# Common up projection for two tiles at a time, and scatter-adds written out with indices read in place

## What is computed

```python
h = patches @ conv_w + conv_b + pos
a = layernorm(h)
h = h + attention(a) + a                 # 12 heads; q and k are layer-normed; softmax
x = layernorm(h)
route_prob = softmax(x @ Ws + bs)        # 9 experts
p, routes = max(route_prob), argmax(route_prob)
out_e = gelu(x @ W1[e] + b1[e]) @ W2[e] + b2[e]          # 192 -> 768 -> 192
common, sel = out_0, out_routes
final = where(routes == 0, common, p * sel + (1 - p) * common)
h = h + final
```

## Time and profile before

| | us |
|---|---|
| median of 3 runs (lowest, highest) | 388.1 (388.03, 388.18) |
| profiled execution, its own time | 386.88 |
| its span in the trace | 385.0 |
| PE busy | 364.3 (95%) |
| POOL busy | 188.3 (49%) |
| DVE busy | 172.2 (45%) |
| ACT busy | 163.9 (43%) |

### The profile page before, as it was taken

One profiled execution on the slowest core, in us unless ns is written; L12 is line 12 of the kernel. 1 busy time (PEld: TensorE's weight loads), 2 busy tenths in 40 slices (PEclk: granted clock), 3 DMA queues, 4 the chain that ended last, 5 costly groups with the idle time before them and its releaser, 6 DMA issues. The chain is left out here.

```text
span 385.0 us, 10445 instructions
## 1 busy us (share of the span) xinstructions
PE 364.3 (95%) x3291; PEld 325.6 (85%) x3292; DVE 172.2 (45%) x595; ACT 163.9 (43%) x553; POOL 188.3 (49%) x307
## 2 busy tenths in 40 slices
PE   6799999999999999899999999998999999999991
PEld 5677877788888888788888899997999999999991
DVE  3365767777777787544232265411112211111111
ACT  0122233333333354778444454335545544555540
POOL 1657977777777787443013006740333333444333
PEclk9999999999999999999999999999999999999997
DMA  7764335353321435435000905626666776676630
GB/s 243 234 207 120 101 105 162 94 156 91 90 79 48 130 113 166 124 97 187 20 0 14 245 2 142 217 80 147 150 170 160 176 187 164 167 165 164 155 76 0
DMA packets 40589, 49.58 MB, mean 129 GB/s; under 512 B 10412, under 2 KB 32313, under 8 KB 40553
## 3 DMA queue, kind: packets, MB, share of 16 engines
q1 hardware_dynamic: 34641, 42.95, 37.8%
q0 software_dynamic: 5024, 5.72, 8.8%
q10 hardware_dynamic: 888, 0.45, 0.4%
HBM read 39.84 MB, written 10.27 MB: 130 GB/s over the span
## 5 line engine op out<-in xcount | busy, mean ns | idle before, releaser
L641 PE MATMUL bank<-W,ARENA 128*128 (+1 forms) x516 | 94.6, 334 | 1.5 <-issue 1.2
L641 PEld LDWEIGHTS bank<-W,ARENA 128*128 128x128 f32 x516 | 82.8, 190 | 5.7 <-issue 1.5
L1371 POOL DMA_INDIRECT out<-ARENA,ID x25 | 39.4, 1575 | 71.3 <-DVE ARENA L1236 62.0
L855 ACT ACTIVATE ARENA<-score_banks,B1R 128x128 f32<-128x128 f32 x150 | 41.5, 376 | 39.8 <-PE score_banks L631 24.1
L855 ACT ACTIVATE ARENA<-score_banks,B1T 128x128 f32<-128x128 f32 x108 | 29.9, 375 | 31.8 <-PE score_banks L631 31.8
L1269 POOL TENSOR_TENSOR VS<-V,R 108x384 f32<-108x384 f32 x32 | 27.7, 865 | 30.5 <-DVE R L960 30.2
L1232 DVE TENSOR_TENSOR ARENA<-bank,B 128x192 f32<-128x192 f32 x25 | 8.9, 358 | 71.6 <-PE bank L641 71.6
L623 PE MATMUL score_banks<-RINGS,W1R 128*128 128x128 f32 x300 | 37.8, 276 | 1.4 <-ACT RINGS L795 0.8
L623 PEld LDWEIGHTS score_banks<-RINGS,W1R 128*128 128x128 f32 x300 | 35.6, 192 | 1.8 <-issue 1.8
L1260 POOL TENSOR_TENSOR RINGS<-QK,GM 128x216 f32<-128x216 f32 x64 | 34.1, 553 | 3.4 <-PE score_banks L579 3.4
L579 PEld LDWEIGHTS score_banks<-QK,RINGS 48*108 48x108 f32 x512 | 28.7, 171 | 6.1 <-issue 2.9
(11 more groups left out here) (149 smaller groups left out, 622.1 us busy)
## 6 DMA issues: line engine op xcount, KB each, us to landing
W1R<-in_w SPq DMA_DIRECT2D x25, 384.0 KB
V<-v_rows SPq DMA_DIRECT2D x96, 54.0 KB
W<-in_w SPq DMA_DIRECT2D x9, 576.0 KB, 4.2
W1R<-in_w_rest SPq DMA_DIRECT2D x50, 96.0 KB
ARENA<-in_patches SPq DMA_DIRECT2D x11, 384.0 KB, 3.6
packed_tokens<-RINGS POOLq DMA_DIRECT2D x1, 2425.0 KB, 13.2
ARENA<-packed_tokens SPq DMA_DIRECT2D x25, 97.0 KB, 2.8
PT<-in_patches SPq DMA_DIRECT2D x6, 384.0 KB, 3.2
```

Source lines behind the costliest of these rows:

```text
L641: last = pe.matmul(bank[2 * par][:, 0:D], HT[par][:, c * P:c * P + P], W2[:, bass.ds((expert * FC + c) * D, D)], start=c == 0, stop=c == F ...
L855: last = act.activation(HT[par][:, to:to + P], bank[6 + g][:, c * P:c * P + P], ACT.Gelu, bias=b1[:, bias:bias + 1])
L1371: pool.indirect_dma_start(out, bass.IndirectOffsetOnAxis(ap=ID[par][:, 0:1], axis=0), YR[par], None, bounds_check=TOKENS - 1, oob_is_err=F ...
```

## The change

From tile 4 on the common up projection works on pairs of tiles (2q, 2q+1), q = 2 to 8, in the even steps 24, 26, ..., 36. Each matmul then has 256 moving columns, the two tiles' rows side by side, for one load of weights. The results take six half banks in banks 4 to 7. In the odd steps 25, 27, ..., 37 there is no up projection. `gelu_pair` takes 256 columns in each of six activations, into buffers twice as long; `common_down` still works on one tile at a time, at its old step. `count_ranks` uses bank 3 in place of banks 4 and 5 and keeps its place. The arena that holds the buffers grows by 112 columns. In the groups' part, POOL's loop is written out, the copy to `ID` and its two waits are gone, and the indirect DMA reads the token numbers from `SLOT_ROWS` directly.

```diff
+PAIR = 2
+ALONE = 4
+ARENA_COLS = 5912
-        ID = [sb(f"ID{i}", 1, I32) for i in range(2)]
-        HT = [cut(DFF) for _ in range(2)]
+        HTP = [cut(PAIR * DFF) for _ in range(2)]
+        HT = [HTP[1][:, i * DFF:(i + 1) * DFF] for i in range(2)]
+        def xn2t_pair(q):
+            both = QK[:, 2 * TOKENS:4 * TOKENS].rearrange("p (u n) -> p u n", u=PAIR)
+            return both[:, :, q * 2 * P:(q + 1) * 2 * P]
+        def pair_chunk(c):
+            b, at = ((bank[6], 0), (bank[6], 1), (bank[4], 0), (bank[7], 0), (bank[7], 1), (bank[5], 0))[c]
+            return b[:, at * PAIR * P:(at + 1) * PAIR * P]
...
 -                ffn_down(n, n % 2, 0)
+                if n < ALONE:
+                    ffn_down(n, n % 2, 0)
+                    return
+                q, u = n // PAIR, n % PAIR
+                for c in range(FC):
+                    if c % (FC // 2) == 0:
+                        pe.wait_ge(gelu_done, 4 * q + 2 + 2 * (c // (FC // 2)))
+                    last = pe.matmul(bank[2 * u][:, 0:D], HTP[q % 2][:, (c * PAIR + u) * P:(c * PAIR + u + 1) * P],
+                                     W2[:, c * D:(c + 1) * D], start=c == 0, stop=c == FC - 1)
+                last.then_inc(y_done, 1)
+            def pair_up(q):
+                pe.wait_ge(gelu_done, 4 * q)
+                pe.wait_ge(s_shifted, STEPS)
+                pe.wait_ge(xn2t_saved, PAIR * q + 2)
+                for c in range(FC):
+                    pe.matmul(pair_chunk(c), W1[:, c * P:c * P + P], xn2t_pair(q)[:, :, 0:P],
+                              start=c % 3 != 1, stop=False, skip_group_check=True)
+            def pair_up_rest(q):
+                for c in range(FC // 2):
+                    at = DFF + c * P
+                    for g in range(2):
+                        rows = slice(g * DB, g * DB + DB)
+                        last = pe.matmul(pair_chunk(g * (FC // 2) + c), W1[rows, at:at + P], xn2t_pair(q)[rows, :, P:2 * P],
+                                         start=False, stop=True, skip_group_check=True)
+                        if c == FC // 2 - 1:
+                            last.then_inc(f1_done, PAIR)
 ...
-                pe.wait_ge(s_shifted, STEPS)
-                pe.matmul(bank[4][:, 0:TE], const("before"), onehot, start=True, stop=True)
-                pe.matmul(bank[5][:, 0:TE], const("ones"), onehot, start=True, stop=True).then_inc(ranks_done, 1)
+                pe.wait_ge(o_copied, STEPS)
+                pe.matmul(bank[3][:, 0:TE], const("before"), onehot, start=True, stop=True)
+                pe.matmul(bank[3][:, 2 * P:2 * P + TE], const("ones"), onehot, start=True, stop=True).then_inc(ranks_done, 1)
 ...
-                if kf is not None:
+                if kf is not None and kf < ALONE:
                     common_up(kf)
+                elif kf is not None and kf % PAIR == 0:
+                    pair_up(kf // PAIR)
 ...
+            def gelu_pair(q):
+                act.wait_ge(y_done, PAIR * q - 2)
+                for g in range(2):
+                    act.wait_ge(f1_done, 4 * q + 2 * g + 2)
+                    for c in range(g * (FC // 2), (g + 1) * (FC // 2)):
+                        last = act.activation(HTP[q % 2][:, c * PAIR * P:(c + 1) * PAIR * P], pair_chunk(c), ACT.Gelu,
+                                              bias=B1T[:, c:c + 1])
+                    last.then_inc(gelu_done, PAIR)
 ...
-            def group_step(i, ks):
-                kh, = ks
-                n, par, half = tile_at(i, kh)
-                if kh >= 2:
-                    pool.wait_ge(y_added[par], 16 * half)
-                pool.tensor_copy(ID[par][:, :], SLOT_ROWS[:, bass.ds(2 * n + 1, 1)].bitcast(I32)).then_inc(id_ready, 1)
-                pool.wait_ge(id_ready, n + 1)
-                pool.wait_ge(y_scaled, n + 1)
-                ride(pool)
-                pool.indirect_dma_start(out, bass.IndirectOffsetOnAxis(ap=ID[par][:, 0:1], axis=0), YR[par], None,
-            two_by_two(pool, group_step, (0,), GROUPS)
+            for n in range(GROUPS):
+                pool.wait_ge(y_scaled, n + 1)
+                ride(pool)
+                row_ids = SLOT_ROWS[:, 2 * n + 1:2 * n + 2].bitcast(I32)
+                pool.indirect_dma_start(out, bass.IndirectOffsetOnAxis(ap=row_ids, axis=0), YR[n % 2], None,
```

More of the change, by code:

```diff
@@ L135, in const @@
             return CST[0:rows, a:b]
-        ARENA = sb("ARENA", 5800)
+        ARENA = sb("ARENA", ARENA_COLS)
         marks = [0]
@@ L143, in cut @@
             marks[0] += n
-            assert marks[0] <= 5800
+            assert marks[0] <= ARENA_COLS
             return ARENA[:, a:a + n]
@@ L717, in main_step @@
                     conv(kc, KC // 2, KC)
-                if kf is not None:
+                if kf is not None and kf < ALONE:
                     ffn_up_rest(kf, xn2t(kf), W1)
+                elif kf is not None and kf % PAIR == 0:
+                    pair_up_rest(kf // PAIR)
                 if s == MIXER_START + TILES + 2:
@@ L872, in main_step @@
                     exp_scores(k_exp, 0, k_exp)
-                if kg is not None:
+                if kg is not None and kg < ALONE:
                     gelu(kg, kg % 2, B1T, kg >= 2)
+                elif kg is not None and kg % PAIR == 0:
+                    gelu_pair(kg // PAIR)
                 if k_o is not None:
@@ L1152, in slots @@
                 dve.wait_ge(ranks_done, 1)
-                then(dve.tensor_copy(by_expert(counts), bank[5][:, 0:TE].rearrange("p (t e) -> p e t", e=EXPERTS)))
+                then(dve.tensor_copy(by_expert(counts), bank[3][:, 2 * P:2 * P + TE].rearrange("p (t e) -> p e t", e=EXPERTS)))
                 then(dve.tensor_tensor_scan(running, const("keep"), counts, 0.0, ALU.mult, ALU.add))
@@ L1164, in slots @@
                 then(dve.tensor_tensor(by_expert(before), by_expert(before), per_e(3).unsqueeze(2).to_broadcast([P, EXPERTS, TILES]), ALU.add))
-                then(dve.tensor_tensor(by_tile(scratch), bank[4][:, 0:TE].rearrange("p (t e) -> p t e", e=EXPERTS),
+                then(dve.tensor_tensor(by_tile(scratch), bank[3][:, 0:TE].rearrange("p (t e) -> p t e", e=EXPERTS),
                                        before.rearrange("p (e t) -> p t e", t=TILES), ALU.add))
@@ L1359, in _ @@
                                         bounds_check=GROUPS * P - 1, oob_is_err=False).then_inc(scattered, 16)
-            def group_step(i, ks):
-                kh, = ks
-                n, par, half = tile_at(i, kh)
-                if kh >= 2:
-                    pool.wait_ge(y_added[par], 16 * half)
-                pool.tensor_copy(ID[par][:, :], SLOT_ROWS[:, bass.ds(2 * n + 1, 1)].bitcast(I32)).then_inc(id_ready, 1)
-                pool.wait_ge(id_ready, n + 1)
-                pool.wait_ge(y_scaled, n + 1)
-                ride(pool)
-                pool.indirect_dma_start(out, bass.IndirectOffsetOnAxis(ap=ID[par][:, 0:1], axis=0), YR[par], None,
-                                        bounds_check=TOKENS - 1, oob_is_err=False,
-                                        compute_op=ALU.add).then_inc(y_added[par], 16)
             pool.wait_ge(slot_rows_in, 16)
@@ L1377, in _ @@
                 pool.wait_ge(out_stored[ring4], 16 * len(range(ring4, TILES, 4)))
-            two_by_two(pool, group_step, (0,), GROUPS)
+            for n in range(GROUPS):
[3 more added lines that the diff above has]
+                pool.indirect_dma_start(out, bass.IndirectOffsetOnAxis(ap=row_ids, axis=0), YR[n % 2], None,
+                                        bounds_check=TOKENS - 1, oob_is_err=False,
+                                        compute_op=ALU.add).then_inc(y_added[n % 2], 16)
 def _consts(np):
```

2 lines of the change are left out of this document (removed).

## The result

The changed kernel takes 396.7 us in the median of 6 runs, against 388.1 us before; run by run on the same chips the ratio is 1.022, with a 95% interval of 1.018 to 1.026. A second set of runs gave 1.023 (1.019 to 1.027). So it is slower by 8.6 us in these medians, not by the 4.7 us forecast, and just outside the range (390.5 to 396.5). The profiled execution took 395.71 us, its span is 393.9 us, 8.9 us longer than before.

The account below looks back on a forecast made before the run. Two paths were taken to meet at the first gather, TensorE's work and the chain behind `count_ranks`; the groups' part was TensorE-bound. `count_ranks` +5.4 and tail -0.7 gave +4.7 us on 388.1: 392.8 us, range 390.5 to 396.5.

Parts of the forecast that it names:

- the pair's length: Paired up projection on TensorE: 4.05 us against 4.60 for two single ones, saving 0.55 us for each of 7 pairs.
- the lower bound that I took: Paired up projection: 3.90 us from below, from the spacing of projections with 384 columns.
- The estimate of 3.93 us: Paired up projection by the skill's matmul spacing rule, doubled: 218 ns for 256 columns; the sum would be 0.5 us smaller.
- steps 24 to 30: Steps up to `count_ranks`: four even steps +1.75 us each, two odd -0.12 each, step 29 -1.33, sum +5.4 us.
- the even step: Steps 24, 26, 28 and 30: the pair replaces one up projection, +1.75 us each.
- the odd one: Steps 25 and 27: 2.30 us removed but `common_down` waits for `add_log` behind the norm, so -0.12 us each.
- `count_ranks` sets the start of the groups: First gather: `count_ranks` moves from 225.53 to 231.0, so the gathers land and group 0 starts 5.4 us later.
- the chain of fixed length: From `count_ranks` over `slots` and 18 scatters at 1.29 us to the gathers: unchanged, so it passes on the 5.4 us.
- no slack is left to soak up any of the delay: First gather: TensorE's 0.3 us wait there was taken to mean the whole 5.4 us delay reaches group 0.
- the tail: Kernel's end: without the copy to `ID` the last add starts earlier, -0.7 us, bounds 0 and 1.1 us.
- the clock's case: Rival, chance 0.18: the clock falls in the idle time ahead of group 0, +3 us, 395.8 us in all.
- The lower bound of my own case, 391.3 us: Whole kernel: lower end of the main forecast's bounds, 391.3 to 395.0 us, given 0.67.

Follow-up runs that it names:

- add_log experiment: The changed kernel with `add_log` ahead of `norm_xn2` on VectorE from step 24 on: 391.2 us, ratio 1.008 to the kernel before.
- adds-only trace: The kernel before with only the written-out scatter-adds, no copy to `ID`: 387.1 us, ratio 0.998.
- late count_ranks: The kernel before, without pairs, with `count_ranks` one step later, behind the up projection of step 31: 391.8 us, ratio 1.012.
- filled kernel: The changed kernel with unread matmuls in TensorE's idle places, in steps 25, 27, 29 and ahead of the first group's transposes: 392.7 us, ratio 1.013.
- count_ranks first: The changed kernel with `count_ranks` at the head of step 30, ahead of the paired projection: 393.7 us, ratio 1.015 to the kernel before.
- both edits of count_ranks in the kernel before: The kernel before with `count_ranks` at the head of step 30 (387.9 us, ratio 1.001), or one step late (391.8 us, ratio 1.012).
- late pairs with count_ranks in place: The changed kernel with pairs only from tile 10 on, `count_ranks` behind the pair of step 30: 389.2 us, ratio 1.005 to the kernel before.
- the early table: The changed kernel with pairs from tile 10 on, `count_ranks` at the head of step 30, GELU table loaded early: 385.8 us, ratio 0.996.
- filled ahead of the gather: The changed kernel with 11 unread matmuls ahead of the first group's transposes alone, none in the odd steps: 394.7 us, ratio 1.019.
- late pairs with count_ranks first: The changed kernel with pairs only from tile 10 on and `count_ranks` at the head of step 30: 386.8 us, ratio 0.998.
- both first: The changed kernel with `add_log` ahead of `norm_xn2` and `count_ranks` at the head of step 30: 386.7 us, ratio 0.998.

## Why the prediction was right in its sign and wrong in its size

**Right: the pair's length.** 4.05 us forecast, 4.18 measured, inside 3.90 to 4.60. The price of 4.17 worked out from the 64 further columns of `common_down` was better than the mean with the lower bound that I took. The estimate of 3.93 us by the rule of the Trainium skill (TensorE: Matmul & The Clock Gate, section "Wait — 56ns, not 53.3ns?") was too low by 0.25 us.

**Right: steps 24 to 30.** The odd steps' wait for `add_log` behind the norm is there (1.71 us, preceded by 0.45 us for `h2_added`), and the add_log experiment took it away. Steps 24 and 25 cost +1.59 us for +1.63 forecast, which is closer than its parts: the even step was +1.88 for +1.75, the odd one -0.29 for -0.12. `count_ranks` is 5.7 us later without the clock, forecast 5.4.

**Right: `count_ranks` sets the start of the groups.** In the six traces in which TensorE stands at the first transpose until the gathers land, or fills that time, the transpose comes 34.0 to 34.2 us behind `count_ranks`: the chain of fixed length. Moved forward, `count_ranks` gave 2.9 us in the changed kernel; moved back, it cost 4.6 us in the one before, where TensorE was late for a reason of its own too.

**Wrong, by 0.87 us: "no slack is left to soak up any of the delay".** I read the 0.3 us that TensorE's weight load waited for the gather as the gather being last. The traces say otherwise: the first transpose comes 2.05 us behind the gathers' issue when it waits for them (265.98 to 268.03), and came 2.8 us behind it before (257.73 to 260.55). The gathers had been there for some 0.8 us, and TensorE was the last. The 0.3 us that I leaned on cost TensorE nothing: the adds-only trace has no such wait and the same 35.02 us from `count_ranks` to the first transpose as before, against the 34.0 to 34.2 us above. What that short wait was is not shown. The late count_ranks in the kernel before shows the same slack from the other side (3.6 for 4.15 us).

**Not in the sum: the gather of the third group.** In the first trace it came late behind the stores and cost 1.84 us. So the rest without the clock is 6.2 us in that trace and 5.0 us in the runs of the filled kernel. That 5.0 is near the 4.7 us forecast is luck in part: in the filled kernel's trace the groups from group 1's up projection to the last bias took 1.35 us more than before (113.13 against 111.78 us), for which the sum has no term, and the slack of 0.87 us goes the other way.

**Right: the tail.** -0.73 us for -0.7.

**Wrong: the clock, put at nothing in the sum.** This is the step that put the time outside the range. I had the mechanism as a rival with 0.18, on the ground that the trace showed one fall, 2.6 us after the last matmul, and priced it at +3 us for one place, the wait ahead of group 0. The idle time I had forecast there (3 us) came (2.6), and both traces of the changed kernel fall to half behind it, as does that of add_log first (2.67 us). What I left out is that the same forecast made three more idle stretches in steps 25, 27 and 29 (0.45 and 1.71, 0.45 and 1.71, 0.89 us), each shorter than 2.6 us. The rival had no term for them. The runs put 2 to 2.5 us on them: filling the gap ahead of the gather alone gives 1.4 to 2 us, filling all of them 3.9 us, where the sum had nothing and the rival 3 us for one place. With my own sum of 4.7 us the clock's case would have been 4.7 + 3.9 = 8.6 us, or 396.7 us. That this is the measured median to the tenth is chance, with 3.9 us known to some 2 us; but the clock's case should have been the forecast and not the rival. Apart from the one near 160 us and the end of the program, every fall to half clock in the traces stands right behind a wait of TensorE: of 1.7 us in an odd step (four traces, in each behind one of the two such waits), of 2.4 to 2.7 us ahead of the gathers (three), of 2.02 us in the late count_ranks. A wait of 1.32 us had none behind it, nor had the filled places. Which waits bring a fall in a given run stays open. The Trainium skill (TensorE: Matmul & The Clock Gate, section "HAM oscillation — how this bites in real kernels") says that waits for transfers let the clock drop, and the windows above agree for the gathers (0.50 behind 2.63 us of idle). I weighed it as a single coincidence.

The lower bound of my own case, 391.3 us, doesn't follow from its terms either: a pair of 3.90 us and a tail of -1.1 us give 388.1 + 4.8 - 1.1 = 391.8.

What stays open: the stretch at half clock near 160 us. It is in the first trace of the changed kernel and in those of the adds alone, add_log first, count_ranks first, filled, both edits of count_ranks in the kernel before, the late pairs with count_ranks in place, and those with the early table, where the work is that of the kernel before at that place; the traces of before, of the changed kernel's second set, of filled ahead of the gather and of the late pairs with count_ranks first haven't it; in the trace of both first it lasts from 159.2 to 189.9 us. In all of them TensorE has just waited 1.4 us for ScalarE (159.34 us in the changed kernel, 159.59 before), so that wait alone doesn't decide it. Since the adds alone and the moves of `count_ranks` touch nothing ahead of 160 us, the change isn't its cause. It adds 1.3 us to the profiled spans that have it.

## What to carry to other kernels

An instruction that a change removes may be the cover of something else. Before taking its time as gained, look in the trace for what runs beneath it on the other engines, in their own order: here a norm stood ahead of a nine-column addition that the next matmul needed. And a long operation that grows, though it saves in total, delays everything queued behind it on its engine; if one of these feeds a chain of fixed length, put it ahead of the operation. Both were moves of three lines, and turned a loss of 9 us into no loss.

Where a forecast says that TensorE will stand idle for some microseconds in a kernel that kept it busy, the clock belongs into the sum, not into the rivals.

## What the runs showed of the hardware

TensorE can gain by doing useless work: filling 2.2 us, 2.2 us, 0.9 us and 2.6 us of waiting with matmuls took 3.9 us off the kernel, and the mean granted clock rose from 0.979 to 0.993. With the waits of steps 25, 27 and 29 left idle it was 0.984.

A paired GELU of 256 columns costs less than two of 128: six of them take 2.30 us in the changed kernel's trace (step 24), against 1.66 us for six with 128 columns.

A gather can be held back by stores that stand ahead of it in the queue's order: the gather of the third group was issued 6.45 us behind the first ones in one trace and 4.64 us in another of the same kernel, because it stands behind stores whose rows wait for earlier stores to land (5.25 us of VectorE's waiting in the first).
